# A perceiver block with a mixture of experts on one core: the wait for the residual, the last low half and VectorE's copies of index columns are put elsewhere in their queues

## The reference

```
x = x + xattn(layernorm(x), ctx)     # 16 heads of 128, rms-normed q and k, softmax, Wo
x = x + attn(layernorm(x))           # 16 heads in chunks of 64, decayed causal mask, gate, o_w
x = x + ffn(layernorm(x))

def ffn(x):                          # 512 tokens, 32 experts, inner width 352
    top_w, top_i = top_k(softmax(x @ gate_w.T), 6)
    y = sum over the 6 of top_w * (silu(x @ w1[e]) * (x @ w3[e])) @ w2[e]
    shared = (silu(x @ sw1) * (x @ sw3)) @ sw2      # two shared halves of width 352
    return y + shared
```

## Time and profile before

| what | us |
|---|---|
| median of 3 runs | 1005.73 |
| lowest and highest of them | 1003.46, 1011.45 |
| the profiled execution, its own time | 1010.82 |
| its span, first to last instruction | 1009.1 |

### The profile page before, as it was taken

The page is one execution under the profiler, slowest core; times in us unless marked ns, Lnnn a source line. Parts: engine busy times, 40 slices in busy tenths (PEclk is TensorE's granted clock), DMA queues, the critical chain, the costliest instruction groups (busy, mean ns, idle before and its releaser), DMA issues.

```text
span 1009.1 us, 18374 instructions
## 1 busy us (share of the span) xinstructions
PE 978.1 (97%) x5548; PEld 843.2 (84%) x5549; DVE 692.0 (69%) x1053; ACT 592.0 (59%) x966; POOL 272.2 (27%) x170
## 2 busy tenths in 40 slices
PE   9999899999999999999999999989999999999997
PEld 7887799989988887888888888767788988788885
DVE  6655665576557765667787675666667888778776
ACT  6544666566666656554555543541366777678773
POOL 2200221222123052223333200010124454454541
PEclk9999999999999999999999999999999999999999
DMA  9100453321231341122221106210588889999995
GB/s 316 49 1 1 119 186 87 104 83 46 79 104 55 83 139 55 61 70 83 83 83 62 42 21 222 77 43 6 209 288 240 293 269 340 351 321 294 305 324 157
DMA packets 76144, 145.09 MB, mean 144 GB/s; under 512 B 13540, under 2 KB 41060, under 8 KB 75856
## 3 DMA queue, kind: packets, MB, share of 16 engines
q1 hardware_dynamic: 68256, 132.53, 39.1%
q0 software_dynamic: 7856, 12.16, 5.4%
HBM read 146.86 MB, written 15.07 MB: 160 GB/s over the span
## 4 chain that ended last, share of the span: by engine, by line
PE 66%; DMA 11%; SPq 8%; issue 7%; DVE 4%; ACT 3%; DVEq 0%; ACTq 0%; POOLq 0%
PE ps L327 17%; PE ps L328 17%; PE ps L329 17%; PE ps L712 6%; DMA w_and_lists<-in_w 4%; SPq L947 3%; DMA w_raw<-in_w 3%; SPq L1186 2%; PE ps L980 2%; PE ps L789 1%; PE ps L779 1%; PE ps L769 1%; SPq L1190 1%; DMA y_scratch<-x 1%; DMA wo_raw<-in_owT 1%
## 5 line engine op out<-in xcount | busy, mean ns | idle before, releaser
L1005 DVE TENSOR_TENSOR w_l<-w_raw,w_h 128x1408 fp32r<-128x1408 f32 x76 | 121.9, 1624 | 35.3 <-ACT w_h L1001 22.7
L1001 ACT ACTIVATE w_h<-w_raw 128x1408 fp32r (+1 forms) x76 | 103.0, 1376 | 41.4 <-DMA w_raw<-in_w 35.1
L741 POOL TENSOR_TENSOR lw_l<-lw_raw,lw_h 128x1024 fp32r<-128x1024 f32 x32 | 77.0, 2412 | 144.8 <-ACT lw_h L737 139.5
L327 PE MATMUL ps<-w_h,xeT_h 128*128 128x352 f32 x288 | 98.3, 341 | 5.9 <-DVE w_l L1005 5.4
L328 PE MATMUL ps<-w_l,xeT_h 128*128 128x352 f32 x288 | 93.8, 326 | 0.0
L329 PE MATMUL ps<-w_h,xeT_l 128*128 128x352 f32 x288 | 93.7, 325 | 0.0
L1161 POOL DMA_INDIRECT xe<-xn_scratch,take x37 | 39.6, 1071 | 192.1 <-DVE give L1109 108.2
L1165 POOL DMA_INDIRECT y_scratch<-ob,give x34 | 81.0, 2382 | 17.6 <-issue 9.7
L327 PE MATMUL ps<-xT_hi,lw_h 128*128 128x512 f32 x192 | 78.0, 406 | 0.0
L328 PE MATMUL ps<-xT_lo,lw_h 128*128 128x512 f32 x192 | 77.1, 402 | 0.0
L329 PE MATMUL ps<-xT_hi,lw_l 128*128 128x512 f32 x192 | 76.0, 396 | 0.0
(11 more groups left out here) (327 smaller groups left out, 2734.4 us busy)
## 6 DMA issues: line engine op xcount, KB each, us to landing
w_raw<-in_w SPq DMA_DIRECT2D x78, 704.0 KB
w_and_lists<-in_w SPq DMA_DIRECT2D x39, 512.0 KB
w_and_lists<-in_w SPq DMA_DIRECT2D x39, 192.0 KB
rkB<-rk_scratch SPq DMA_DIRECT2D x56, 128.0 KB, 3.2
wq_raw<-in_Wq SPq DMA_DIRECT2D x8, 512.0 KB, 5.0
wo_raw<-in_Wo SPq DMA_DIRECT2D x16, 256.0 KB, 2.9
lw_raw<-in_kwT SPq DMA_DIRECT2D x8, 512.0 KB, 3.3
lw_raw<-in_qwT SPq DMA_DIRECT2D x8, 512.0 KB, 3.4
```

The source lines that it names most:

```text
L327: nc.tensor.matmul(out_ap, lh, rh, start=first, stop=False)
L741: e.tensor_tensor(lw_l[n][:, :, :], lw_raw[n][:, :, :], lw_h[n][:, :, :], ALU.subtract).then_inc(lw_ready[n], 1)
L1001: e.activation(w13_h[:, k, n, :, :], w13_raw[:, slot(raw), n, :, :], ACT.Copy).then_inc(w13_hi_s, 1)
L1005: e.tensor_tensor(w13_l[:, k, n, :, :], w13_raw[:, slot(raw), n, :, :], w13_h[:, k, n, :, :], ALU.subtract).then_inc(w13_ready, 1)
```

## The change

Four edits. In `ex_dve` the copies to take and give leave their place ahead of h and stand behind the low halves of w1 and w3, ahead of that of w2. Take is made one pass sooner (item m+4 in pass m, behind a wait for PE's transpose of item m+2), and give too (item m-1 in pass m, from pass 1 on). Take of item 3 stays in pass 0, and the last two passes make no take. On POOL the wait for IO_X moves from ahead of the gather of ex_pool(2) to behind it, ahead of the scatter. The low half of the last item's result moves ahead of all four sums.

```diff
--- before.py
+++ after.py
@@ -1132,24 +1132,27 @@
         def ex_dve(e, i, k, own, ahead=None, last=False):
 
             m = i * 2 + k
-            if last:
-                ex_dve_give(e, ahead, k)
             if not isinstance(m, int) or m > 0:
                 ex_dve_hT_low(e, m - 1, 1 - k)
             if last:
                 homes(e, i)
             if not last:
                 ex_dve_xT(e, m + 1, 1 - k)
-                ex_dve_take(e, m + 3, 1 - k)
+            if isinstance(m, int) and m == 0:
+                ex_dve_take(e, 3, 1)
             if isinstance(i, int) and i == 0:
                 ex_dve_x(e, NSH - 2 + k)
-            elif not last:
-                ex_dve_give(e, i - 1 if ahead is None else ahead, k)
             ex_dve_h(e, k, m + NSH)
             raw = None if last else raw_slot(e, m + 1)
             if not last and (not isinstance(m, int) or m > 0):
                 ex_dve_w13(e, 1 - k, 0, m * 2 + 7, raw)
                 ex_dve_w13(e, 1 - k, 1, m * 2 + 8, raw)
+            if not last:
+                if ahead is None:
+                    e.wait_ge(xeT_ps, m + 3)
+                    ex_dve_take(e, m + 4, k)
+                if not isinstance(m, int) or m > 0:
+                    ex_dve_give(e, i if k == 1 else i - 1 if ahead is None else ahead, 1 - k)
             ex_dve_w2(e, m, k, own)
             return raw
 
@@ -1179,6 +1182,8 @@
             e.wait_ge(take_ready, m + 4)
             e.sem_inc(acc_turn, 1)
             ex_gather(e, 1 - k)
+            if isinstance(m, int) and m == 2:
+                e.wait_ge(scratch_io, IO_X)
             if not isinstance(i, int) or i > 0:
                 ex_pool_scatter(e, i - 1, k)
 
@@ -1455,8 +1460,6 @@
             e.wait_ge(take_ready, 3)
             ex_gather(e, 0)
             for m in range(4):
-                if m == 2:
-                    e.wait_ge(scratch_io, IO_X)
                 ex_pool(e, m // 2, m % 2)
             with e.Fori(2, last_i) as i:
                 ex_pool(e, i, 0)
@@ -1962,11 +1965,10 @@
             ex_dve(e, last_i, 1, raw, ahead_i, last=True)
             ex_dve_hT_low(e, last_i * 2 + 1, 1)
             ex_dve_ob_low(e, last_i, 0)
+            ex_dve_ob_low(e, last_i, 1)
             e.wait_ge(y0_in, 16)
             e.wait_ge(scratch_io, IO_X)
             for t in range(TT):
-                if t == 2:
-                    ex_dve_ob_low(e, last_i, 1)
                 e.wait_ge(part_arrived[t], 32)
                 e.tensor_tensor(x[:, t, :], y_back[0][:, t, :], y_back[1][:, t, :], ALU.add).then_inc(y_sum, 1)
             for t in range(TT):
```

## The result

The changed kernel took 1004.78 us (median of 14 runs), the kernel before 1008.53 us (median of 14 runs beside them): a ratio of 0.997 with a 95% interval of 0.9956 to 0.9984. (One of the 14, of 1951.79 us, was disturbed: the ratio leaves it out, and without it the median is 1004.68.) The profiled execution took 1004.89 us, its span is 1003.1 us. Everything lies inside 1%.

What follows compares the result with a forecast made beforehand. PE, busy 97% of the span, was taken as the bound, with weights' arrival setting the pace in starved stretches. Early 3.0 + loop 0 + end 2.0 = 5.0 us off the 1005.73 us median gave 1000.7 us, range 995.5 to 1006.0.

Steps and rivals of the forecast that it cites:

- What bounds the kernel: Expert stretch: PE 97% busy, setting the pace in places, weights' arrival in others; a late gather of item 5 stalls PE.
- Part 1: Early items: IO_X wait behind the gather frees item 5's gather; net gain 3.0 us, ends 0 and 3.4.
- what is late next: End of ex_dve(3): item 2's give waits for scatter 0, delaying w2_low and hT_l; PE loses 0 to 0.7 us, taken 0.4.
- the gross term: Early items, before give's loss: stall of 1.68 us and low clock's loss of 1.69 us go, together 3.4 us.
- Part 2: Copies moved in the loop: cost 0, with PE's waits covering them; ends -5 us and +10 us.
- I take 0 for the loop: Loop: earlier gathers and scatters fit before DVE must wait, ACT's scatter waits go but give nothing; net 0 us.
- Part 3: Kernel's end: earlier last scatter and ob_l(1), PE's 3.0 us wait goes, DVE ends last; gain 2.0 us.
- I keep it whole: After the early items: the 3.0 us lead survives to the end, as weight loads have room; other end, nothing kept.
- Rival 1: Only the end gains: gather lands late or the starved stretch swallows the 3 us; 1003.7 us, chance 0.18.
- Rival 2: Loop slower: give's wait for the scatter of its slot takes over; 1019.6 us, chance 0.05.
- Rival 3: Earlier gathers and scatters leave DMA engines free for weights; half of 11.8 us goes too; 994.8 us, chance 0.09.
- rival 4: Nothing for PE: gather as late as before, DVE's give eats the end's gain; 1005.7 us, chance 0.08.

Runs made afterwards that it cites:

- the two repeats: The changed kernel, unaltered, run again in two later series: 1005.46 us, ratio 0.9999, and 1003.75 us, ratio 0.9989 to the kernel before.
- e2_wait: Kernel before with only POOL's wait for IO_X moved behind the gather; 1003.22 us, ratio 0.9967.
- e4_wait_tail: Kernel before with the IO_X wait behind the gather and the last low half ahead of the sums, copies unmoved; 1002.92 us, ratio 0.9974.
- e5_copy1: Changed kernel with x written into the other half of y_scratch and the IO_X wait ahead of scatter 1; 1001.88 us, ratio 0.9965.
- f2_give_old: Changed kernel with x in y_scratch's other half, IO_X wait ahead of scatter 1, and give alone back ahead of h; 1004.03 us, ratio 0.9953.
- e3_copies: Changed kernel with the IO_X wait and the last low half put back, so only the copies are moved; 1008.24 us, ratio 1.0012.
- e8_copy1_old_copies: Kernel before with IO_X wait behind the gather, ahead of scatter 1, x in y_scratch's other half, last low half moved, copies unmoved; 1000.15 us, ratio 0.9948.
- the kernels with copy 1 and old copies: Three runs of one code: x in y_scratch's second half, wait and end changed, take and give copied ahead of h as before; ratios 0.9948, 0.9957, 0.9951.
- f1_held_pool: Changed kernel with x in y_scratch's other half, IO_X wait ahead of scatter 1, POOL's gather held until DVE made xeT_l; 1005.86 us, ratio 0.9963.
- e6_light_before: Kernel before with loads of w1 and w3 cut to 64 of 128 rows from item 7 on; 1018.85 us, ratio 1.0148.
- f4_copy1_old: Same code as e8_copy1_old_copies, repeated on another chip; 1004.7 us, ratio 0.9951 to the kernel before.

## Why the prediction was right and where it was wrong

What bounds the kernel: right. The gather of item 5 left the path once its wait was moved. It started at 743.30 in a trace whose front is 2.14 us ahead, so at 745.4 by the clock of the kernel before, where I had 745.5. PE's wait for xe went, and the clock stayed at 1.00.

Part 1, "what is late next": the mechanism was right, its size wrong, and this is the first step that failed. I had PE losing 0 to 0.7 us to give's wait for scatter 0 and took 0.4; it lost 2.03. By the clock of before, PE was ready at 761.3 (I had 761.4). Three terms were too small. The write of x took 11.47 us and not 10.28, now with the gather beside it: 1.2 us more, where I had allowed 0 to 0.7 and in effect used the middle. So scatter 0 started at 752.8 where I had 751.56 to 752.26 (the 0.9 us from the write's end to POOL's start are in both). It then took 8.57 us to give's release where I had 8.1. So give came at 761.4 in place of 759.7 to 760.4. And from give to PE's start it took 1.9 us (759.23 to 761.15), where I had 1.7. Against the middle of my figures that is 0.9 + 0.5 + 0.2, nearly the whole 1.6 us between 0.4 and 2.03. Of 3.4 us gross 1.4 stayed. The same held in the two repeats: PE's waits for hT_l were 1.9 and 2.5 us. ACT's path through ob and w_h I had overlooked. Without the moved copies it takes their place: from item 2 to item 8 PE lost 3.5 us by it in e2_wait and 0.6 in e4_wait_tail, against 2.2 to 2.8 us in the three traces of the changed kernel (all over the 41.44 of the undisturbed ones). e5_copy1 shows the gross term itself to be right.

Part 2, "I take 0 for the loop": wrong, and the second step that failed. The copies cost 2.0 ± 1.0 us, and f2_give_old points at that of give; why it costs stays open. What I had argued was seen: DVE has no wait for scatters in the loop, ACT's waits are gone, hT_l is not waited for in starved items. The effects on POOL were also those of the rule I had cited from the Trainium skill (GPSIMD Engine Reference, Key points): scatters beside hT_l and h are issued faster (2.50 to 1.59 us), gathers beside w2_low slower (1.05 to 1.26 us). I had said that neither moves the sum, and for the scatters f2_give_old bears that out: it has the short issues (1.59 us) and the time of the kernel with the long ones. In the traces the cost shows up faintly and in two places. With new copies the stretch from the last transpose to the first ob_h took 16.1 us (mean of eight traces, 15.3 to 16.8), with old ones 15.5 (seven, 15.2 to 15.9). From item 6 to the last transpose it was 209.0 against 208.1 us; there single executions range from 205 to 212 us, so one trace says nothing. With the 0.4 us that the end gains by them (below) these make 1.1 of the 2.0 us. Whether the transfers that now start sooner push back weights is argued, not shown.

Part 3, the end: right in its steps, and a little too large as a sum. DVE did become what ends last, with ob_l(1) within 0.8 us of ob_h(1) and the last add ending 5.5 us after it. The first trace gave 2.4 us against my 2.0, but over all traces the stretch from the first ob_h fell from 14.5 us (three, with the old end and old copies) to 13.1 (seven with full loads, new end and new copies), so 1.4; in most of the seven DVE still waited for parts of y_back, up to 1.3 us; and the 0.6 us that the item before it loses belongs to the same account. Each half of the part is worth about 1 us alone: the earlier ob_l 1.0 us (13.5 in five traces with give where it was, where the sums then wait for y_back), the earlier give 1.1 in the one trace that has it alone (13.34 in e3_copies). Together they gave 1.4, so they do not add up in full.

"I keep it whole": the lead of the early part reaches the end in kernels with old copies. e8_copy1_old_copies and its repeats gain 5.1 us, where the early part (31.35 to 27.6) and the end (14.5 to 13.5) make 4.7. Rival 1 comes nearest to the size of the result but not by its way: the gather was in time, and the kernels with copy 1 and old copies kept their lead, within 0.9 us; the gain was eaten at scatter 0 and by the copies. Rival 2 (which Part 2 prices at 10 us and the list of rivals at 18.9 less 5) occurred only in f1_held_pool, in 8 waits of at most 1.2 us. Rival 3 did not occur: w_l's waits are 12.0 against 11.8 us. Nor did rival 4: PE's wait for xe went.

The account then is 1.4 (early) + 1.4 - 0.6 (end) - 0.9 (middle, uncertain) = 1.3 us, against 1.4 ± 0.9 measured and 5.0 forecast. (The early 1.4 is that of one pair of traces; from item 2 to item 8, three with the wait unmoved and old copies took 45.3 us on average, from 44.25 to 46.35, and the three of the changed kernel 43.8.) The first series looked kinder, 3.75 us by its medians and 2.5 by its means. And the 1005.73 from which I had reckoned 1000.7 was the median of three runs; 14 runs of the same kernel gave 1008.53. That 1004.78 lies inside my range of 995.5 to 1006.0 is in part luck: the range was wide enough for no change at all.

## What to carry to other kernels

When a wait is moved behind another instruction, work out the transfer that it now holds as carefully as the one that it frees, with its slower landing beside new neighbours, and list every engine that writes into a buffer which that transfer reads, not only the one that was edited. Look next for the reason of the wait: with x written where the first scatter does not add, that scatter no longer held up anything in the first items (in time this was worth 1.2 ± 1.2 us). And a copy of 0.15 us that starts transfers is not priced by its own length; moved together with useful edits it can cost a part of their gain, so time it by itself on the same chip.

## What the runs showed of the hardware that I had not expected

- Half the rows did not make the loads cheaper for the DMA engines. From 860 to 880 us they moved 207 GB/s at a share of 1.05 with w1 and w3 loaded to 64 partitions, 354 at 1.04 with 128.
- The granted clock did not follow the length of a stall. It fell to 0.64 behind a wait of 1.68 us (before) and 0.58 behind 1.31 (e2_wait), a mix of 1.2 and 2.4 GHz, but stayed at 1.00 behind 2.03 us in the changed kernel. Nor does the place of the stall decide: in e6_light_before PE stopped at the same instruction as in the kernel before, behind the transposes of h, waited 2.29 us for xe, and the clock stayed at 1.00. So one trace does not tell what the clock will do behind a stall in the next.
- The issue of a scatter on POOL takes 1.6 or 2.5 us by what DVE does beside it. The queue's engine time per MB was lower in the traces with the long issues (2.22% against 2.37%), but f2_give_old, with short ones, has 2.27%.
- Executions differ by more than all that this change does: e8_copy1_old_copies and f4_copy1_old are one code and took 205.0 and 212.4 us from item 6 to item 35 (on two chips); one series of the kernel before, on one chip, runs from 1000.06 to 1011.04 us.
